# Attention and expert layers on one core: row maxima applied two score groups later

## The reference

```python
def attention(x, ...):                       # 16 heads of 16 channels
    q, k, v = (split_heads(lin(x, W, b)) for W, b in ((Wq, bq), (Wk, bk), (Wv, bv)))
    rel = rel_emb[r[None, :] - r[:, None] + 511]          # (1024, 1024, 16), indices clamped
    qk = einsum('bhld,bhrd->bhlr', q, k) / 4
    qk = qk + einsum('bhld,lrd->bhlr', q, rel)
    out = einsum('bhlr,bhrd->bhld', softmax(qk), v)
    return lin(out, Wo, bo)

x = x + layernorm(attention(layernorm(x), ...))
x = x + layernorm(ffn(layernorm(x), ...))    # base + shared low rank + 6 experts, the best 2 weighted
```

## Time and profile before

| | us |
|---|---|
| median of three runs | 6338.6 (6333.1 to 6343.19) |
| the profiled execution, its time | 6342.86 |
| the profiled execution, its span | 6341.1 |
| PE busy | 5961.8 (94%) |
| DVE busy | 4987.0 (79%) |
| POOL busy | 3652.9 (58%) |
| ACT busy | 3127.8 (49%) |

### The profile page before, as it was taken

How to read it: one execution, slowest core, us unless ns; L and a number is a source line. 1 busy time by engine, 2 the same in 40 slices (tenths; PEclk the granted TensorE clock), 3 DMA queues, 4 the chain that set the end, 5 groups by cost and what they waited for, 6 DMA issues and landing times.

```text
span 6341.1 us, 408511 instructions
## 1 busy us (share of the span) xinstructions
PE 5961.8 (94%) x178176; PEld 5617.6 (89%) x178176; DVE 4987.0 (79%) x10289; ACT 3127.8 (49%) x5145; POOL 3652.9 (58%) x4709
## 2 busy tenths in 40 slices
PE   5999999999999999999999999999999999999997
PEld 4989899899998998898999899899999999998987
DVE  3787788878788887878887888888788788887786
ACT  1555455455555554555555555455555555554554
POOL 5555655565565555555655655555565556556555
PEclk7999999999999999999999999999999999999998
DMA  3111121111212112121121211112111121211211
GB/s 87 39 44 52 36 61 36 54 44 38 60 36 62 36 36 62 36 61 34 42 58 36 60 37 49 47 40 60 36 53 45 36 60 40 59 37 36 62 36 27
DMA packets 570090, 296.74 MB, mean 47 GB/s; under 512 B 384177, under 2 KB 534689, under 8 KB 568625
## 3 DMA queue, kind: packets, MB, share of 16 engines
q1 hardware_dynamic: 568624, 272.86, 16.0%
HBM read 184.46 MB, written 88.60 MB: 43 GB/s over the span
## 4 chain that ended last, share of the span: by engine, by line
PE 83%; DVE 8%; issue 4%; DVEq 3%; POOLq 1%; ACT 1%; POOL 0%; SPq 0%; DMA 0%
PE sc L667 22%; PE pw L693 15%; PE sc L683 14%; PE sc L662 13%; PE pm L714 4%; PE pw L700 4%; PE pw L714 4%; PE pm L674 4%; DVE r L962 3%; DVEq L973 2%; DVE y2n L928 2%; DVE nm L971 1%; PE pm L727 1%; PE pm L705 1%; DVE gate L1005 1%
## 5 line engine op out<-in xcount | busy, mean ns | idle before, releaser
L962 DVE TRANSPOSE_TENSOR_REDUCE r<-sc 128x32 f16<-128x1024 f32 x2048 | 2548.8, 1245 | 52.0 <-PE sc L667 51.4
L667 PE MATMUL sc<-rm,tw 96*128 96x32 f16 x65536 | 2293.4, 177 | 71.6 <-issue 70.8
L847 ACT ACTIVATE prob<-sc 128x1024 f32<-128x1024 f32 x2048 | 2097.3, 1024 | 193.7 <-PE sc L683 141.3
L667 PEld LDWEIGHTS sc<-rm,tw 96*128 96x128 f16 x65536 | 1979.9, 97 | 79.5 <-issue 79.0
L662 PE MATMUL sc<-qm,ks 96*128 96x64 f16 x32768 | 1639.8, 193 | 28.8 <-DMA ks<-qk_s 15.5
L971 DVE TENSOR_REDUCE nm<-pm 16x32 f16<-16x256 f32 x2048 | 840.8, 411 | 753.7 <-PE pm L674 750.3
L662 PEld LDWEIGHTS sc<-qm,ks 96*128 96x128 f16 x32768 | 1302.8, 98 | 34.3 <-issue 34.2
L683 PE MATMUL sc<-nmm,pick 128*128 128x64 f16 x32768 | 1302.0, 193 | 2.5 <-DVE nmm L974 1.2
L683 PEld LDWEIGHTS sc<-nmm,pick 128*128 128x128 f16 x32768 | 1151.9, 98 | 122.4 <-issue 105.5
L693 PE MATMUL pw<-prob,vs 128*32 128x128 f32 x32768 | 1115.7, 277 | 129.8 <-DVE nm L971 124.7
L693 PEld LDWEIGHTS pw<-prob,vs 128*32 128x32 f32 x32768 | 842.6, 110 | 185.8 <-DVE nm L971 137.4
(11 more groups left out here) (131 smaller groups left out, 5803.9 us busy)
## 6 DMA issues: line engine op xcount, KB each, us to landing
raw<-qk_s SPq DMA_DIRECT2D x774, 64.0 KB, 2.8
tw<-tw_s SPq DMA_DIRECT2D x512, 72.0 KB, 2.1
v_s<-vpad SPq DMA_DIRECT2D x136, 256.0 KB, 3.6
vs<-v_s SPq DMA_DIRECT2D x64, 512.0 KB, 3.7
ks<-qk_s SPq DMA_DIRECT2D x384, 64.0 KB, 2.5
xin<-x SPq DMA_DIRECT2D x138, 128.0 KB, 2.9
qk_s<-qkh SPq DMA_DIRECT2D x272, 64.0 KB, 1.7
qk_s<-qkl SPq DMA_DIRECT2D x272, 64.0 KB, 1.6
```

Source lines behind the costliest of these rows:

```text
L667: last = mm(out3[:, :, 2 * k:2 * k + 2], tw[:, jp, u:u + P], rm[:, i, k, :, :], start=False, stop=False, skip_group_check=True)
L847: A(prob[:, jp % 2, :, :, i * IW:(i + 1) * IW], sc[:, 2 * buf:2 * buf + 2, :].rearrange("p c (h i) -> p c h i", i=IW), ACT.Exp).then_inc(s ...
L962: v.tensor_reduce(r1[:, 0:2 * H], sc[:, 2 * buf:2 * buf + 2, :].rearrange("p c (h i) -> p (c h) i", i=IW), axis=AX.X, op=ALU.max, apply_tr ...
```

## The change

- `shift` and the exponential of a group come two groups behind its scores (`LAG = 2`), and `shift` stands between block 0 and block 1 of the group that PE works on, no longer behind `wide` and `mixed`.
- The transposition of the maxima moves from ahead of block 1 to within it, between its content and its relative part.
- `wide` and `mixed` stand ahead of block 0. `pv` stands at k = 3 of the next stage and k = 0 of the one after it, `transpose_parts` at k = 1, projections at k = 2.
- The turned maxima of a stage move from k = 1 to k = 2 and to columns of `pm` of their own (`p_nm`).
- PE waits for `s_nmr` only ahead of k = 2 and of the groups in `MIXED`, and for the group before the last.
- On DVE, `side` stands between `maxima` and `spread` of the same group; two of its pieces move (nmin and dm from g = 1 to 3, rden and o from 7 to 8). ACT's copies follow their producers.

```diff
+LAG = 2
+MIXED = (1, 3, 9, 10, 11, 12)
...
+        p_nm = pm[:, 4 * P - H:4 * P]
...
-                if g == 0 and b:
+                if g == 1 and b:
                     pe.wait_ge(s_xn1, t - 1)
                     transpose2(p_t, xn1).then_inc(s_x1Tp, 1)
...
-                if g == 8 and a:
+                if g == 9 and a:
                     pe.wait_ge(s_o, t)
...
             def wide(t, n, g, att, proj, a):
 
                 jp, k = divmod(g, NI)
-                if k and (a if jp == 0 else att):
-                    pj = (jp - 1) % NJP
-                    if k == 1:
...
-                        pv(pj, 0)
-                    elif k == 2:
-                        pv(pj, 1).then_inc(s_pv, 1)
-                    else:
-                        transpose_parts(t * NJP + jp - 1)
-                if k == 0 and jp < 3 and proj:
-
-                    if a if jp == 0 else att:
+                if k == 0 and (a if jp < 2 else att):
+                    pv((jp - 2) % NJP, 1).then_inc(s_pv, 1)
+                if k == 1 and (a if jp < 2 else att):
+                    transpose_parts(t * NJP + jp - 2)
+                if k == 2 and jp < 3 and proj:
+
+                    if a if jp < 2 else att:
                         pe.wait_ge(s_part, t * NJP + jp - 1)
...
+                if k == 3 and (a if jp == 0 else att):
+                    pj = (jp - 1) % NJP
+                    pe.wait_ge(s_exp, t * NG + NI * jp)
...
+                    pv(pj, 0)
...
             def tile(t, n, att, proj, a, b, ph=None):
                 read = None
                 for g in range(NG):
                     jp, k = divmod(g, NI)
-                    old = a if g == 0 else att
+                    turned = k == 2 and (a if jp == 0 else att)
+                    wide(t, n, g, att, proj, a)
+                    if (turned or g in MIXED) and (a if g < LAG else att):
+                        pe.wait_ge(s_nmr, t * NG + g - 1)
+                    read = mixed(t, g, a, b)
+                    if turned:
+                        mm(p_nm, nm[:, (jp - 1) % 2, :], ident16[:, 0:H], start=True, stop=True).then_inc(s_nmtp, 1)
...
                         free = t * NG + g - NBUF + 1
                         if not (isinstance(free, int) and free <= 0):
                             pe.wait_ge(s_exp, free)
-                        scores(g, 0, buffer(ph, g))
+                        content(g, 0, buf)
+                        rel(g, 0, buf)
+                    if a if g < LAG else att:
+                        shift(buffer(ph, g - LAG), t * NG + g - 1)
+                    if att:
+                        content(g, 1, buf)
                     if read is not None:
                         pe.wait_ge(*read)
-                    if old:
+                    if turned:
+                        pe.wait_ge(s_nmt, t * NJP + jp)
+                    if a if g < 1 else att:
                         transpose_max(t * NG + g)
                     if att:
-                        scores(g, 1, buffer(ph, g)).then_inc(s_scores, 1)
-
-                    wide_first = k == 1 or g in (0, 8)
-                    if wide_first:
-                        wide(t, n, g, att, proj, a)
-                    if old:
-                        pe.wait_ge(s_nmr, t * NG + g)
-                    read = mixed(t, g, att, a, b)
-                    if not wide_first:
-                        wide(t, n, g, att, proj, a)
-                    if old:
-                        shift(buffer(ph, g - 1), t * NG + g)
+                        rel(g, 1, buf).then_inc(s_scores, 1)
...
                     if a if g == 0 else att:
+                        maxima(buffer(ph, g - 1), t * NG + g)
+                    side(g, t, n, proj, a, b)
+                    if a if g == 0 else att:
                         spread((g - 1) % NG, t * NG + g)
-                    if att:
-                        maxima(buffer(ph, g), t * NG + g + 1)
-                    side(g, t, n, proj, a, b)
```

More of the change, by code:

```diff
@@ L653, in _, with content, rel @@
             pe.wait_ge(s_cdve, 1)
-            def scores(g, c, buf):
+            def content(g, c, buf):
                 jp, i = divmod(g, NI)
                 bank = sc[:, 2 * buf + c, :]
-                out3 = bank.rearrange("p (h i) -> p h i", i=IW)
                 j = (2 * jp + c) * P
                 for h in range(H // 2):
-                    last = mm(bank[:, 2 * h * IW:(2 * h + 2) * IW], ks[:, h, j:j + P],
-                              qm[:, i, 2 * h:2 * h + 2, :].rearrange("p h i -> p (h i)"),
-                              start=(h == 0), stop=False, skip_group_check=True)
+                    mm(bank[:, 2 * h * IW:(2 * h + 2) * IW], ks[:, h, j:j + P],
+                       qm[:, i, 2 * h:2 * h + 2, :].rearrange("p h i -> p (h i)"),
+                       start=(h == 0), stop=False, skip_group_check=True)
+            def rel(g, c, buf):
+                jp, i = divmod(g, NI)
+                out3 = sc[:, 2 * buf + c, :].rearrange("p (h i) -> p h i", i=IW)
                 for k in range(IW // 2):
@@ L719, in both, with mixed @@
                 return [(lambda i, c=c: lhs[:, i, c, cols], lambda j, c=c: rhs[:, j, c, :]) for c in range(2)]
[L721 to L729, removed]
-                if g == 0 and b:
+            def mixed(t, g, a, b):
+                if g == 1 and b:
                     pe.wait_ge(s_xn1, t - 1)
@@ L794, in wide @@
                         product(pw[:, 0:D], *both(xT2, w_v2)).then_inc(s_vp, 1)
+                if k == 3 and (a if jp == 0 else att):
+                    pj = (jp - 1) % NJP
+                    pe.wait_ge(s_exp, t * NG + NI * jp)
+                    pe.wait_ge(s_vs[pj], batch_of(t - 1 if jp == 0 else t) * 16 + 16)
+                    if proj and jp < 3:
+                        pe.wait_ge((s_xT, s_qkf, s_vf)[jp], n + 1)
+                    else:
+                        pe.wait_ge(s_part, t * NJP + jp - 1)
+                    pv(pj, 0)
             def tile(t, n, att, proj, a, b, ph=None):
@@ L861, in tile @@
                     old = a if jp == 0 else att
-                    if k == 1 and old:
+                    if k == 2 and old:
                         act.wait_ge(s_nmtp, stage + 1)
@@ L866, in tile @@
                             act.wait_ge(s_dm, t)
-                        copy(nmt[:, pj, :], p_n[:, 0:H]).then_inc(s_nmt, 1)
-                    if g == 0 and b:
+                        copy(nmt[:, pj, :], p_nm).then_inc(s_nmt, 1)
+                    if k == 0 and (a if jp < 2 else att):
+                        act.wait_ge(s_pv, stage)
+                        copy(ot[:, :, :].rearrange("p c i -> p (c i)"), pw[:, :]).then_inc(s_ot, 1)
+                    if k == 1 and (a if jp < 2 else att):
+                        act.wait_ge(s_ott, stage)
+                        if jp == 2 and a:
+                            act.wait_ge(s_wp, t)
+                        copy(parts[:, (jp - 2) % NJP, :, :],
+                             pw[:, :].rearrange("p (h d) -> p h d", d=32)[:, :, 0:17]).then_inc(s_part, 1)
+                    if g == 1 and b:
                         act.wait_ge(s_x1Tp, t - 1)
@@ L882, in tile @@
                         copy(y20[:, :], p_t).then_inc(s_y20, 1)
-                    if g == 2 and a:
+                    if g == 4 and a:
                         act.wait_ge(s_dm, t)
@@ L888, in tile @@
                         A(eg[:, :], lg[:, :], ACT.Exp, bias=nlm[:, 0:1], accum_out=gsum[:, :]).then_inc(s_eg, 1)
[L890 to L899, removed]
+                    if g == 2 and proj:
                         act.wait_ge(s_xTp, n + 1)
                         copy(xT[:, :, :].rearrange("p c i -> p (c i)"), pw[:, 0:2 * P]).then_inc(s_xT, 1)
-                    if g == 4 and proj:
+                    if g == 6 and proj:
                         act.wait_ge(s_qkp, n + 1)
@@ L905, in tile @@
                         copy(qkf[:, :, :].rearrange("p e i -> p (e i)"), pw[:, :]).then_inc(s_qkf, 1)
-                    if g == 8 and proj:
+                    if g == 10 and proj:
                         act.wait_ge(s_vp, n + 1)
@@ L909, in tile @@
                         copy(vf[:, :], pw[:, 0:D]).then_inc(s_vf, 1)
-                    if g == 8 and a:
+                    if g == 9 and a:
                         act.wait_ge(s_oTp, t)
                         copy(oT[:, :, :].rearrange("p c i -> p (c i)"), p_t).then_inc(s_oT, 1)
-                    if a if g == 0 else att:
+                    if a if g < LAG else att:
                         before(g, t, ph)
@@ L977, in side @@
             def side(g, t, n, proj, a, b):
-                if g == 1 and a:
+                if g == 3 and a:
                     dve.wait_ge(s_nmt, t * NJP)
@@ L1018, in side @@
                     v.tensor_reduce(rank[:, :], cadd[:, :, :], axis=AX.X, op=ALU.add)
-                if g == 7 and a:
+                if g == 8 and a:
                     dve.wait_ge(s_osum, t)
```

12 lines of the change are left out of this document (4 added, 8 removed).

## The result

The changed kernel takes 6566.7 us (median of four runs, 6558.22 to 6571.27) against 6339.07 us in the same comparison: 1.0358 times, 95% interval 1.034 to 1.0376, so 228 us slower. The prediction said slower, 6622 us, range 6430 to 6725. The mean granted TensorE clock is 0.974 to 0.977 in the four runs, where the kernel before had 0.985.

What follows compares the result with a forecast made beforehand. PE was taken to be bound by its own work and waits for DVE's `nm`. 4.2 us added less 1.94 removed gave +2.25 us a tile, 284 us over 126 tiles: 6622 us, range 6430 to 6725.

Steps and rivals of the forecast that it cites:

- What bounds the kernel: PE's waits for DVE's `nm`, ahead of `pv` (124.7 us) and `transpose_parts` (53.9 us), once per tile each.
- the second finding: A small DVE operation that starts inside a POOL operation is held to its end, as `cgt`, `gate` and `nmm` were.
- What the change removes: Stalls ahead of `pv` (1.07), ahead of `transpose_parts` (0.57) and at other groups (0.3): 1.94 us a tile can go.
- Exponentials: Block 0 waits for the exponential three groups back, at g = 2, 5 and 13: 0.36 us a tile added.
- Group 14: PE waits at the turned maxima of the stage, behind `s_nmr` of group 12: 0.6 us added.
- Groups 5 to 7: Held `gate` and `cgt` stall PE 1.6, the next maxima 0.35, operations beside POOL's split 0.8: 2.75 us, before 1.07.
- The open term of 0.8: Group 7, `ceqt`, `cadd` and the masked copy held by POOL's three operations on `qkf`: 0 to 1.1 us, taken as 0.8.
- The sign of being right that asked for over 0.5 us of `cadd`: DVE's `cadd` would last over 0.5 us if the forecast was right.
- Elsewhere: Masked copies held around g = 15 to 2 delay the maxima behind them: 0 to 1.0 us a tile, taken as 0.5.
- The sum: 4.2 us added, 1.94 removed: +2.25 us a tile, 284 us over 126 tiles.
- `gate` passes: Rival: in group 5 only `ceq` is held by `wp`; 1.6 shrinks to 0.2, 6446 us; chance 0.21 with other mild losses.
- The slack pays: Rival: POOL misses DVE's small operations altogether, only 0.36 and 0.6 stay; -0.98 us a tile, 6215 us; chance 0.07.

Runs made afterwards that it cites:

- three experiments: Kernel before, three separate runs: POOL waits for `cgt` ahead of the query/key split, 6246.1 us; POOL waits for `rank`, 6236.2 us; `ceq` and `cgt` one group later, 6274.1 us.
- the half exponential: Changed kernel with the exponential over key block 0 only, 512 elements a lane in place of 1024: 6564.0 us.
- the turned maxima were moved: Changed kernel with the turned maxima of a stage, and their wait for `nm`, moved behind the shift of the same group: 6708.7 us.
- without `wp`: POOL's `wp` and its two additions cut to 16 elements each: 6301.8 us in the changed kernel, 6242.4 us in the kernel before.
- the same cure on the new order: Changed kernel where POOL waits for DVE's `cgt` ahead of `wp`, nothing left out: 6472.9 us.

## Why the prediction was right

**What bounds the kernel.** Right, and the second finding more so than the first: the held operations of the earlier trace rows were both the old stall (three experiments took it away by moving POOL or DVE) and most of the new loss. Two things in it were too wide. Not every small operation is held: `rg`, one element with one input, ran its 0.12 us inside `wp` (3124.30). And the 0.42 us of `gate`, as its 1.43 us now, say that it was held; in which mode VectorE ran it no run here shows.

**What the change removes.** Counted 1.07, 0.57 and 0.3; measured 1.12 and 0.55, and the small ones. (`s_nmr` is waited for at nine groups, not eight; no term used it.)

**Exponentials.** Counted 0.36 us a tile, measured 0.49 as stalls. But the step failed as a term of the sum: it has to be taken out, since the half exponential changed the time by 3 us, less than the runs differ. DVE's chain is as long and takes the waits over.

**Group 14.** Counted 0.6, measured 0.51. That the exponential waits behind it, nearly as late, came out only when the turned maxima were moved.

**Groups 5 to 7.** Counted 1.6 at the turned maxima, measured 1.39, since `wp` took 2.04 us and not 2.24 (the last section has why), so `gate` was let go earlier. Counted 0.35 at the maxima behind them, measured 0.35. The open term of 0.8 was mis-sized: it was 0 by the medians. I had said that `cadd` loses nothing if it slips into a gap between two POOL operations; it did, at 3129.95, 0.08 us ahead of `qkh`. The sign of being right that asked for over 0.5 us of `cadd` failed with it. This term alone is 0.8 x 126 = 101 us, more than the 55 us by which the forecast was high.

**Elsewhere.** Counted 0.5 for held masked copies; the stalls there are 0.7 us in all, not all of them held copies. The clock was put at nothing: the stretches at half clock add about 0.3 us a tile. They follow the stalls, 25 of the 59 the new one of group 6, and most of what was added went again without `wp`.

**The sum.** 2.25 us a tile said, 1.48 measured by the medians and 1.76 on the mean. That the mean lies as near is in part luck: the terms that were too high (0.8, and 0.2 at the turned maxima) were offset by the clock and by what was counted too low elsewhere.

**Rivals.** "`gate` passes" is refuted by its 1.43 us. "The slack pays" was tried as far as it could be, without `wp`: the changed kernel was then 265 us faster, but the kernel before gained 88 on its own chip too and stayed ahead. Its condition, no small operation held at all, was not met, since the masked copies beside `rm` were still held.

## What to carry to other kernels

Where a short operation of VectorE takes many times its usual length, look which GpSimd operation ends with it, and count a change of order by which pairs it brings together, not only by waits removed. Add slack and then ask what two neighbouring stalls hide from each other: here two waits (the exponential, the turned maxima) stood one behind the other, and taking one away paid nothing. The cheap cure was to let the engine with time to spare wait for the small operations of the other, one semaphore, 1.5%; the same cure on the new order moved the holding to the next operation, and 1.1 of the 1.4 us won at the one stall were lost at others. And look at the granted clock beside the stalls: a stall of 1.4 us was sometimes followed by a stretch at half clock, so that it cost more than its own length.

## What the runs showed of the hardware that was not expected

`wp`, the same POOL instruction on the same shape, took 2.20 us on the mean before and 2.04 after, while the two additions behind it kept their times. The traces show why: the holding goes both ways. In the kernel before, DVE's `xn`, an operation on 256 elements a lane, starts just ahead of `wp`:

```profile
3019.98 0.36 DVE L928 TENSOR_SCALAR xn<-xin,mv,rs 128x256 f32<-128x256 f32 x1
```

and `wp` of the earlier trace rows starts at 3020.01 and takes 2.24. This is so in 126 of 127 tiles: `xn` starts 0.03 to 0.12 us ahead, and `wp` takes 0.11 to 0.20 us over 2.04. In the one tile where `wp` came first, by 0.10 us, `wp` took its 2.04 and `xn`, 0.36 us otherwise, was held for 2.09:

```profile
169.88 2.04 POOL L580 TENSOR_TENSOR wp<-parts,wst 128x1088 f32<-128x1088 f32 x1 [1.25 <-ACT parts L839]
169.98 2.09 DVE L928 TENSOR_SCALAR xn<-xin,mv,rs 128x256 f32<-128x256 f32 x1
```

With `wp` cut to 16 elements, in the kernel before, it took 0.23 us where it came first and 0.34 to 0.42 behind `xn`, so the addition is a wait and not a slower pace. In the changed kernel no `xn` stands there.

And `gate`, six elements a lane with one large input and a scalar, was held to the end of `wp` (1.43 us in place of 0.23) in 127 of 128 tiles, just like the operations with two inputs.
